# Output projections one step sooner behind the key projections, and the low part of the turned tile ahead of the scaled key

## What is computed

```python
x = x + L0(x, cond_512)   # modulated k projection, attention, modulated output projection
x = x + L1(x, cond_512)   # weight of rank 30, made from the condition
x = x + L2(x, cond_512)   # modulated 512 x 512 layer, clipped
x = x + L3(x, ids, ...)   # six blocks of layer norms and table rows, two-layer MLP, layer norm
# in L0, per token, over its 16 heads of 32 features (q = k = v = kx):
scores = einsum('bnhd,bnjd->bnhj', q, k) / sqrt(D)
out = einsum('bnhj,bnjd->bnhd', softmax(scores), v)
out = modulated_linear(out, s, o_aff_w, o_aff_b, o_w, o_b)
```

## Time and profile before

| | |
|---|---|
| median of 3 runs | 1013.16 us (1007.46 to 1014.13) |
| profiled execution | 1011.57 us, span 1009.8 us, granted clock 0.994 of full speed |
| PE busy | 979.1 us, 97% of the span, 6566 matmuls |
| DVE, ACT, POOL busy | 662.7, 489.9, 693.9 us |
| DMA | 125.10 MB, mean 124 GB/s |

### The profile page before, as it was taken

How to read it: one execution, slowest core, us unless ns; L and a number is a source line. 1 busy time by engine, 2 the same in 40 slices (tenths; PEclk the granted TensorE clock), 3 DMA queues, 4 the chain that set the end, 5 groups by cost and what they waited for, 6 DMA issues and landing times.

```text
span 1009.8 us, 18145 instructions
## 1 busy us (share of the span) xinstructions
PE 979.1 (97%) x6566; PEld 782.0 (77%) x6566; DVE 662.7 (66%) x1213; ACT 489.9 (49%) x766; POOL 693.9 (69%) x634
## 2 busy tenths in 40 slices
PE   9989999999999999899999999999999999999995
PEld 5566777777787677788888887888888888888884
DVE  6697767689868878665656557567557556664542
ACT  2798777777777545333342433233334324323231
POOL 5656676676665449777777777768768777777861
PEclk9999999999999999999999999999999999999998
DMA  9634654554422562333232332332233233223220
GB/s 280 229 121 155 226 202 148 178 208 156 143 66 64 188 221 86 107 107 120 76 107 88 109 128 86 109 115 80 81 112 111 78 96 130 66 90 107 79 76 22
DMA packets 58269, 125.10 MB, mean 124 GB/s; under 512 B 7891, under 2 KB 12117, under 8 KB 57156
## 3 DMA queue, kind: packets, MB, share of 16 engines
q1 hardware_dynamic: 46404, 81.98, 24.0%
q0 software_dynamic: 11776, 41.95, 13.4%
HBM read 105.96 MB, written 17.95 MB: 123 GB/s over the span
## 4 chain that ended last, share of the span: by engine, by line
PE 73%; POOL 9%; issue 6%; DVE 6%; DMA 3%; ACT 2%; SPq 1%; POOLq 0%; DVEq 0%; ACTq 0%
PE ps L592 36%; PE ps_y L599 7%; PE ps_k L680 7%; PE ps_o L599 5%; PE tp L604 4%; PE ps_v L633 2%; PE ps_s L665 2%; PE ps_u L700 1%; PE ps_t L713 1%; DMA x_in<-in_x_turned 1%; PE tp L913 1%; POOL h L1810 1%; PE ps_vt L660 1%; DMA xb<-in_x_wide 1%; POOL tt L1818 1%
## 5 line engine op out<-in xcount | busy, mean ns | idle before, releaser
L1796 POOL TENSOR_TENSOR rstd<-var_eps,half 128x1 f32<-128x1 f32 x95 | 53.6, 564 | 105.3 <-DVE var_eps L1561 104.6
L1193 ACT ACTIVATE g_out<-ps 128x512 f32<-128x512 f32 x32 | 19.1, 597 | 170.5 <-PE ps L998 170.5
L1015 ACT ACTIVATE at_diag<-at 32x512 f32<-32x512 f32 x128 | 80.5, 629 | 18.8 <-DVE at L1354 17.5
L1740 POOL TENSOR_TENSOR om<-om,bc 128x512 f32<-128x512 f32 x32 | 41.3, 1292 | 68.1 <-DVE om L1324 68.0
L1727 POOL TENSOR_SCALAR xb<-xb,bias_o 128x512 f32<-128x512 f32 x32 | 52.9, 1652 | 43.6 <-DMA xb<-in_x_wide 43.5
L1567 DVE TENSOR_SCALAR shift_n<-mean_var,rstd 128x1 f32<-128x1 f32 x96 | 20.5, 214 | 94.1 <-POOL rstd L1796 91.8
L1015 ACT ACTIVATE k_diag<-kt 32x512 f32<-32x512 f32 x128 | 80.1, 626 | 1.1
L1147 ACT ACTIVATE h<-h,shift_n,rstd 128x512 f32<-128x512 f32 x32 | 26.1, 817 | 84.6 <-DVE shift_n L1567 84.6
L1547 DVE TENSOR_TENSOR t_lo<-tp,t_hi 128x512 fp32r<-128x512 f32 x64 | 43.8, 685 | 30.0 <-ACT t_hi L1143 30.0
L680 PE MATMUL ps_k<-wk_hi,xh 128*128 128x512 f32 x128 | 54.1, 423 | 0.6 <-DVE xl L1368 0.6
L592 PE MATMUL ps<-wx_high,x_hi 128*128 128x512 f32 x128 | 53.2, 415 | 0.0
(11 more groups left out here) (296 smaller groups left out, 3194.5 us busy)
## 6 DMA issues: line engine op xcount, KB each, us to landing
raw<-in_dec_w SPq DMA_DIRECT2D x30, 512.0 KB, 5.1
x_in<-in_x_turned SPq DMA_DIRECT2D x32, 256.0 KB, 5.0
xb<-in_x_wide SPq DMA_DIRECT2D x32, 256.0 KB, 4.7
x_dram<-xb SPq DMA_DIRECT2D x32, 256.0 KB, 3.8
xt<-x_dram SPq DMA_DIRECT2D x8, 1024.0 KB, 7.9
out<-o SPq DMA_DIRECT2D x32, 256.0 KB, 2.0
raw<-in_int_W SPq DMA_DIRECT2D x7, 1024.0 KB, 6.1
id_rows<-in_id_rows SPq DMA_DIRECT2D x32, 64.0 KB
```

Of the source, the lines that this page charges most:

```text
L1015: last = nc.scalar.activation(dst[g, :, q, :], src[g, :, :], ACT.Copy)
L1740: nc.gpsimd.tensor_tensor(om[:, :], om[:, :], bc[:, STYLE_O, t // TB, :], ALU.mult).then_inc(mix_step, 1)
L1796: nc.gpsimd.tensor_tensor(rstd[:, k:k + 1], var_eps[:, k:k + 1], half[:, :], ALU.pow).then_inc(norm_step[k], 1)
```

## The change

Four edits. The projections run seven steps behind (O_AT = 7), so steps 7 to 38 have one, and step 39 has none; the loads of `xb`, POOL's bias product, `x1_end` and the stores follow, being placed by O_AT, and the last store now falls into attend 39. DVE makes the low part of the turned tile ahead of the scaled key instead of behind it. The three table copies move from the end of step 7 to its middle, ahead of DVE's sum, since the bank that they read is written by step 7's projection. Chunks 0 and 1 each move one step ahead: chunk 0 in front of attend 35, chunk 1 in front of attend 36; chunks 2 and 3 stay.

```diff
@@ order
     yield "attend", T + 2
     if engine != "PE":
         yield "low_rank", 0
+    yield "chunk", 0
     yield "attend", T + 3
-    yield "chunk", 0
+    yield "chunk", 1
     yield "attend", T + 4
     if engine == "SP":
         yield "refine", -2
     yield "split", "x"
-    yield "chunk", 1
     yield "attend", T + 5
@@ body
-    O_AT = 2 * G
+    O_AT = 2 * G - 1
@@ SP, split(n)
                 if n == "s":
-                    for p in range(3):
-                        count = len(range(p, T, 3))
-                        if p == (T - 1) % 3:
-                            sp.wait_ge(x1_ready, T)
-                            sp.dma_start(x1_dram[GROUPS - 1, :, C - 1, :], xb[p][:, :]).then_inc(x1_stored[p], 16)
                     sp.wait_ge(o_done, T)
@@ DVE, attend(s, has)
                     nc.vector.transpose(om[:, :].rearrange("p (h a c) -> p h a c", h=H, c=2),
                                         ps_v[:, :, :, :].rearrange("p a h c -> p h a c")).then_inc(mix_step, 1)
+                if s == O_AT:
+                    table_rows_t(1)
                 if s == T + 1:
                     low_o(s - 4)
...
                 if s == T + 1:
                     x1_end(s)
+                if has(4) and s not in (T + 1, T + 3):
+                    low_o(s - 4)
                 if has(0):
                     dve.wait_ge(k_done, s + 1)
...
                     nc.vector.tensor_tensor(kb[:, :], ps_k[:, :], bc[:, DEMOD_K, s // TB, :], ALU.mult).then_inc(k_step, 1)
-                if has(4) and s not in (T + 1, T + 3):
-                    low_o(s - 4)
@@ DVE, prepare(s)
-                if s == 7:
-                    table_rows_t(1)
```

## The result

The changed kernel took 1023.76 us (median of 4 runs, 1022.41 to 1025.0), the kernel before 1011.88 us beside it (4 runs, 1007.46 to 1014.13). The ratio is 1.0118, with a 95% interval of 1.0091 to 1.0145: slower by 11.9 us. The forecast was 1021.6 (1014 to 1027). The profiled execution took 1025.0 us, its span is 1023.2, 13.4 more than the span before.

A forecast was written before the change was run, and what follows sets the result against it. PE is busy nearly throughout, so PE's work plus its waits was taken as the bound; +1.28 + 0 + 4.9 + 0 + 2.73 + 1.1 = +10.0 us on the profiled 1011.57 gave 1021.6 us, range 1014 to 1027.

The forecast's parts named there:

- Step 7: Step 7's added output projection costs PE its full 2.72 us; table copies ahead of the low part add 0.4 us.
- Step 9: The at_diag wait of 1.44 us at the start of step 9 goes, as first block loads are issued sooner.
- Step 39 gives nothing: Removing step 39's projection gains 0, since PE then waits about as long for DVE's chain before the first x product.
- Steps 11, 15, 19, 27: In these group steps the first projection waits 0.30 us each for the low part made in the same step.
- Step 23: The low part comes late behind DVE's 3.13 us product; PE waits 3.44 us before the projection, 2.5 us net loss.
- Step 31: The group's first projection waits 0.8 us for the low part made in the same step.
- Chunk 0 and the adjoining projections: Chunk 0, ahead of step 35, waits 2.73 us for z; projections adjoining in steps 36 and 37 cost 1.1 us.
- Rival 1: Longer PE waits also cost clock: two falls to half clock on top of the forecast, 1025 us; chance 0.27.
- the 1.44 us wait did nothing: Argument against the clock rival: the existing at_diag wait at the start of step 9, 1.44 us, brought no clock fall.
- Rivals 2 and 3: Rival 2: waits absorbed, step 39 frees PE, 1016.5 us, chance 0.18; rival 3: low part ahead removes waits, 1002.6 us, 0.05.

The follow-up runs named there:

- e2: The kernel before with only the low part of the turned tile put ahead of the scaled key, still eight steps behind; 1013.25 us, ratio 1.0026.
- e10: The kernel before with only the first three residual blocks loaded one step sooner; 1010.54 us, ratio 0.9992.
- e5: The changed kernel with no projection in step 37 and the last two in steps 38 and 39, eight steps behind at the end; 1026.75 us, ratio 1.0131.
- e3: The changed kernel with chunks 0 and 1 back in their old places; 1021.11 us, ratio 1.0100.
- e8: The changed kernel with unused matmuls filling step 23's wait (13) and chunk 0's wait for z (11); 1021.92 us, ratio 1.0107.
- e4: The changed kernel with DVE's 3.13 us product over a weight block moved one step later; 1020.18 us, ratio 1.0089.
- e1: The changed kernel with the low part of the turned tile behind the scaled key again; 1033.48 us, ratio 1.0207.
- e9: The changed kernel with chunks 0 and 1 in their old places and DVE's 3.13 us product one step later; 1019.72 us, ratio 1.0076.
- e7: The kernel before with the low part ahead, DVE's 3.13 us product one step later and three residual blocks loaded sooner; 1008.82 us, ratio 0.9982.
- e11: The same kernel as e7, run again against the kernel before; 1010.40 us, ratio 0.9979.

## Why the prediction held, and where it was off

The direction held, the time lay in the range, 2.2 us over the forecast, and each wait came where it was said. The outcome was the one of over 1%, though, to which the prediction gave 0.40 against 0.54 for no change that can be told.

Part of the closeness is luck. Measured without falls, the terms below add up to 2.57 - 1.67 + 0.91 + 2.31 + 0.72 + 3.79 = 8.6 us, where the sum had 10.0: it was 1.4 too high. Two falls that it had put at nothing add 3.0 in the profiled execution. That makes 11.6, near the 11.9 between the medians; only one execution of the changed kernel was traced, so that its other runs have the same two falls is not shown.

- **Step 7** was to pay 2.72 + 0.4; it paid 2.57. The low part ahead by itself shortens this step from 8.64 to 8.44 us (e2), and against that the product costs 2.77. So the table copies and the wait for the low part cost next to nothing there.
- **Step 9** was to give back 1.44, and gave 1.67; e10 shows the cause named, with 1.65.
- **Step 39 gives nothing**: -0.02 us, as said. e5 shows that the cover is DVE's chain and how easily it breaks to the worse.
- **Steps 11, 15, 19, 27**: 0.30 each was computed, 0.21, 0.22, 0.21 and 0.27 measured; the reciprocal's 0.25 us overlaps the start of the next instruction by 0.08, which I had counted in full.
- **Step 23**: 2.5 for the wait; 2.31 (e3) and 2.32 (e8) without a fall of the clock, 3.70 with a fall (2.31 + 1.4). e4 shows the 3.13 us product as its cause.
- **Step 31**: 0.8; 0.72.
- **Chunk 0 and the adjoining projections**: 2.73 + 1.10 = 3.83; 3.79 with the waits filled (e8), 5.38 with the fall.
- **Rival 1**, the clock, was given 0.27 and half of it came true: the trace has falls behind two of the three waits it named, at 1.4 and 1.6 us each, as it priced them (1.6). The step that failed is that "the 1.44 us wait did nothing" was taken as a reason to put the clock at 0 in the sum: the new waits were up to twice as long. The time lies between the forecast and that rival, 1023.8 between 1021.6 and 1025, nearer the rival. The Trainium skill (TensorE: Matmul & The Clock Gate, "What's actually happening") has inactivity bring the throttled state back, and by that rule the rival was the forecast; the windows above agree, with half clock behind 3.06 and 2.40 us of waiting. It is no certainty: the same trace has a wait of 2.60 us for `fl` with no fall, and e3 one of 3.02.

Not foreseen: the +2.32 us before step 7 in the profiled pair, although the first key product starts 2.47 us sooner than before (13.46 against 15.93). The changed kernel's trace has two falls there that the trace before does not have, of some 1.5 us each. One, at 30 to 34 us, stands behind a wait of 1.72 us for `k_diag`; e1 and e10, with the low part in its old place, have that wait as well (1.73 and 1.69), so it is not made by the change. The other stands behind the wait for `at_diag` that the second edit makes longer (see e2):

```profile
61.10 1.94 PE L628 MATMUL ps_v<-at_diag,v 128*32 128x128 f32 x32 [1.94 <-ACT at_diag L1010]
...
62.00:64.00 2.00, 2.00 (x23) 1.39 (x16) 1.88 (x4) 2.00 (x5) 0.10 (x1) 0.50 0.97 357
```

e3, e4, e5, e8 and e9 are the same program up to step 7. e3, e4 and e8 have no fall at 61 us and reach step 7's key product at +0.05, +0.10 and +1.03 us against before; e5 and e9 have it and stand at +2.50 and +1.35. So this is a cost that comes in some executions, and the sum had no term for it.

Rivals 2 and 3 fell: no wait was absorbed, and e2 shows that the low part ahead frees nothing on balance at eight steps.

## What to carry to other kernels

Count products, and then look at where the schedule has slack: a product taken from a stretch that another engine's chain bounds gives nothing, while the stretch that takes it in pays in full. When a pipeline's lag is cut to the step that makes the input, check every group step, since one large side job on the producing engine (here 3.13 us) sets the worst wait. A new long wait of PE is to be priced with a fall of its clock as a chance, here 1.4 to 1.6 us on top of 2.3 to 3.8. And two waits joined into one longer wait may cost more than the two did, though their sum is the same.

## What the runs showed of the hardware

The scatter of one and the same program goes with the granted clock. Among 13 runs of the kernel before beside one set of experiments, the mean granted clock ran from 0.988 to 0.998, and the correlation of clock and time is -0.89; in two other sets, of 17 and 23 runs, it is -0.65 and -0.82. From the 13 runs:

```
granted clock 0.997: 1008.54 us   0.993: 1009.94, 1011.05, 1011.40 us   0.988: 1014.57 us
```

Six us lie between the ends, though the instructions are the same. The clock is not all of it, since runs at 0.993 differ by 1.5 us.

Behind a long wait a fall is frequent, not certain. These are the waits that several of the twelve traces share, with how many have a fall in them or within 2 us behind:

| wait of PE | us | with a fall |
|---|---|---|
| `at_diag`, at about 60 us | 1.94 to 1.95 | 4 of 9 |
| `at_diag`, at about 79 us | 1.60 to 1.62 | 0 of 9 |
| `ol`, step 23 | 3.02 to 3.61 | 3 of 4 |
| `z`, chunk 0 | 2.40 | 4 of 4 |
| `fl` | 2.60 | 2 of 6 |
| `t_lo`, second refine step | 1.65 to 1.88 | 2 of 4 |
| `t_lo`, second refine step | 3.08 to 3.49 | 7 of 8 |

A fall needs no idle time either: in the trace before, one came at 297 us behind matmuls of two columns. Eight of the twelve traces have one at this place, the changed kernel's among them, and four (e2, e7, e8, e11) do not, with the same matmuls.

In e8 a fall stood behind the next long wait, the one left unfilled. That filling two waits moved it there is not shown, since e1 has a fall at the same place with nothing filled.
